# Cross-attention, second layer: the softmax denominators from a split, rounded sum, one key tile later

## What is computed

```python
q = rmsnorm((hidden_states @ Wq).reshape(B, Sq, H, D), gq)
k = rmsnorm((encoder_hidden_states @ Wk).reshape(B, Skv, H, D), gk)
v = (encoder_hidden_states @ Wv).reshape(B, Skv, H, D)
scores = jnp.einsum('bqhd,bkhd->bhqk', q, k) * scale
attn = jax.nn.softmax(scores, axis=-1)
out = jnp.einsum('bhqk,bkhd->bqhd', attn, v)
```

## Time and profile before

| | before |
|---|---|
| median of 3 runs | 2175.83 us |
| profiled execution, its own time | 2174.4 us |
| its span, first to last instruction | 2172.6 us |
| mean granted TensorE clock | 0.998 |
| second layer's attention | about 1397 to 1980 us of the span |
| one batch of it (sums to sums) | 34.3 to 34.4 us |

### The profile page before, as it was taken

The page is one execution under the profiler, slowest core; times in us unless marked ns, Lnnn a source line. Parts: engine busy times, 40 slices in busy tenths (PEclk is TensorE's granted clock), DMA queues, the critical chain, the costliest instruction groups (busy, mean ns, idle before and its releaser), DMA issues. The chain is left out here.

```text
span 2172.6 us, 27566 instructions
## 1 busy us (share of the span) xinstructions
PE 2110.9 (97%) x8962; PEld 1571.2 (72%) x8962; DVE 1575.4 (73%) x2592; ACT 972.9 (45%) x2593; POOL 1409.9 (65%) x1120
## 2 busy tenths in 40 slices
PE   7999999999999999999999988999999999999999
PEld 7777777777777777777777556666666666665998
DVE  4889888898889888988896642556665666652677
ACT  3444445545454445444545337544444344431432
POOL 1468776887778777877787237187878787771221
PEclk9999999999999999999999999999999999999999
DMA  3000000000000000000001410011011111101110
GB/s 132 29 15 16 29 29 15 21 23 29 15 29 15 29 19 25 15 29 29 15 10 40 140 46 1 29 43 57 29 57 30 56 49 37 43 1 52 37 52 25
DMA packets 15136, 75.63 MB, mean 35 GB/s; under 512 B 1746, under 2 KB 2114, under 8 KB 13986
## 3 DMA queue, kind: packets, MB, share of 16 engines
q1 hardware_dynamic: 14994, 73.89, 10.4%
HBM read 72.97 MB, written 0.92 MB: 34 GB/s over the span
## 5 line engine op out<-in xcount | busy, mean ns | idle before, releaser
L612 POOL TENSOR_TENSOR l_prod<-l_prod 125x256 f32<-125x256 f32 x576 | 417.4, 738 | 270.4 <-DVE l_prod L677 269.7
L677 DVE TENSOR_TENSOR l_prod<-l_side,xq 125x512 f32<-125x512 f32 x576 | 394.9, 686 | 56.2 <-PE l_side L809 48.3
L954 POOL TENSOR_TENSOR l_acc<-l_acc,l_probs 125x896 f32<-125x896 f32 x160 | 346.0, 2162 | 81.7 <-ACT l_probs L904 66.0
L553 ACT ACTIVATE l_probs<-l_slots,mask_bias 125x448 f32<-125x448 f32 x384 | 237.8, 632 | 340.6 <-PE l_slots L748 340.5
L974 DVE TENSOR_TENSOR l_scaled<-l_slots,rk 125x896 f32<-125x896 f32 x192 | 207.0, 1085 | 197.8 <-PE l_slots L1039 197.7
L606 POOL TENSOR_TENSOR l_acc<-l_acc,l_probs 125x896 f32<-125x896 f32 x160 | 338.6, 2116 | 0.0
L535 ACT ACTIVATE l_prod_act<-l_prod_act 125x128 f32<-125x128 f32 x768 | 228.0, 298 | 235.3 <-DVE l_prod_act L677 235.3
L904 ACT ACTIVATE l_probs<-l_scaled 125x896 f32<-125x896 f32 x192 | 182.8, 952 | 320.7 <-DVE l_scaled L974 296.8
L686 DVE TENSOR_REDUCE l_msq<-l_prod 125x4 f32<-125x256 f32 x576 | 235.0, 410 | 1.7
L640 DVE SCALAR_TENSOR_TENSOR top<-l_side,mask_bias,top 125x448 f32<-125x448 f32 x330 | 223.4, 677 | 6.8 <-PE l_side L792 5.8
L1037 PE MATMUL l_slots<-l_qhi,l_clo 128*125 128x448 f32 x384 | 203.0, 529 | 1.4 <-DVE l_qlo L979 1.4
(11 more groups left out here) (258 smaller groups left out, 4487.9 us busy)
## 6 DMA issues: line engine op xcount, KB each, us to landing
land<-in_ctxT SPq DMA_DIRECT2D x32, 750.0 KB, 4.3
l_nat<-in_ctxN SPq DMA_DIRECT2D x16, 750.0 KB
post_we<-in_experts SPq DMA_DIRECT2D x20, 384.0 KB, 3.0
spare<-in_ctxN SPq DMA_DIRECT2D x8, 750.0 KB
nat<-in_ctxN SPq DMA_DIRECT2D x8, 750.0 KB
spare<-in_wo SPq DMA_DIRECT2D x2, 2048.0 KB, 8.5
spare<-in_wqT SPq DMA_DIRECT2D x4, 512.0 KB, 9.2
mid_fac<-in_factors SPq DMA_DIRECT2D x1, 2048.0 KB, 8.2
```

The source lines that it names most:

```text
L553: act.activation(P[t % NP][:, HALF * i:HALF * i + HALF], bank_of("S", t, i)[0:KT, 0:HALF], ACT.Exp, bias=m.mask_bias[:, b, t:t + 1]).then_ ...
L612: pool.tensor_tensor(buf[:, :, 0:C // 2], buf[:, :, 0:C // 2], buf[:, :, C // 2:C], ALU.add).then_inc(s.half_sum, 1)
L677: dve.tensor_tensor(to[:, :, :], bank, xt.unsqueeze(1).to_broadcast([KT, 4, C]), ALU.mult).then_inc(s.side_dve, 1)
L954: pool.tensor_tensor(acc[:, :], acc[:, :], P[t % NP][:, :], ALU.add).then_inc(s.acc, 1)
```

## The change

The denominators are no longer taken from acc by a plain float32 matmul. ScalarE rounds acc to float32r (acc_hi), GpSimd subtracts to get the remainder (acc_lo), and TensorE makes two float32r matmuls for each half, with a float32r block of ones (one). On ScalarE the rounding stands behind exp of tile 1 of the next batch and ahead of `values_out`; on GpSimd the remainder stands ahead of `low_parts` and the adds of the next batch; on TensorE `sums` moves from step 0 to step 1, and on VectorE `invert` and `normalise` from steps 0 and 1 to steps 1 and 2.

```diff
         acc = sb("acc", [KT, QW], F32)
+        acc_hi, acc_lo = sb("acc_hi", [KT, QW], F32R), sb("acc_lo", [KT, QW], F32R)
+        one = sb("one", [KT, 128], F32R)
...
+            def sum_high(b):
+
+                act.wait_ge(s.acc, (NT - 1) * (b + 1))
+                need(act, s.den, b)
+                act.activation(acc_hi[:, :], acc[:, :], ACT.Copy).then_inc(s.acc_hi, 1)
...
                     for bt, tt in tile_ahead(LAG, b, t):
                         exp(bt, bt % 2, tt)
+                sum_high(b)
                 values_out(b)
...
             high_parts(0, 0)
+            act.activation(one[:, :], m.ones[0:KT, :], ACT.Copy).then_inc(s.one, 1)
...
                 if t == 1:
 
-                    need(pool, s.den, b)
+                    need(pool, s.acc_lo, b)
                     pool.tensor_tensor(acc[:, :], P[0][:, :], P[1][:, :], ALU.add).then_inc(s.acc, 1)
...
+            def sum_low(b):
+
+                pool.wait_ge(s.acc_hi, b + 1)
+                need(pool, s.den, b)
+                pool.tensor_tensor(acc_lo[:, :], acc[:, :], acc_hi[:, :].bitcast(F32), ALU.subtract).then_inc(s.acc_lo, 1)
...
                     if t == (6 if b == 0 else 0) and nxt:
                         low_parts(b + 1, 1 - par)
+                sum_low(b)
...
-                    if t == 0 and not start:
+                    if t == 1 and not start:
                         invert(b - 1)
-                    if t == 1 and not start:
+                    if t == 2 and not start:
                         normalise(b - 1)
...
             def sums(b):
 
-                pe.wait_ge(s.acc, (NT - 1) * (b + 1))
+                pe.wait_ge(s.acc_lo, b + 1)
+                pe.wait_ge(s.one, 1)
                 need(pe, s.inv, 2 * b)
...
                 for half in range(2):
-                    last = pe.matmul(norm_banks[:, half, 0:HALF], m.ones[0:KT, :], acc[:, HALF * half:HALF * half + HALF],
-                                     start=True, stop=True)
+                    cols = slice(HALF * half, HALF * half + HALF)
+                    pe.matmul(norm_banks[:, half, 0:HALF], one[:, :], acc_lo[:, cols], start=True, stop=False)
+                    last = pe.matmul(norm_banks[:, half, 0:HALF], one[:, :], acc_hi[:, cols], start=False, stop=True)
                 last.then_inc(s.den, 1)
...
-                        if half == 1 and t == 0 and not start:
+                        if half == 1 and t == 1 and not start:
                             sums(b - 1)
```

More of the change, by code:

```diff
@@ L842, in second_attention @@
         "ld_land", "ld_nat0", "ld_nat1", "ctx_hi", "ctx_lo", "q_hi", "q_lo", "scores", "scaled", "probs", "pv", "acc",
-        "den", "inv", "o_raw", "o_done", "fold_pe", "fold_act", "fold_dve", "y_pe", "y_act"])
+        "one", "acc_hi", "acc_lo", "den", "inv", "o_raw", "o_done", "fold_pe", "fold_act", "fold_dve", "y_pe", "y_act"])
     LAG, NP = 2, 3
```

## The result

The changed kernel takes 2190.95 us (median of four runs, 2189.8 to 2193.53) against 2175.79 before (the three runs given above and one more): ratio 1.0072, 95% interval 1.0056 to 1.0088. It is 15.2 us slower, where +13.65 was forecast; the forecast time was 2189.5. The profiled execution took 2191.12 us with a span of 2189.3, 16.7 over the 2172.6 of before.

What follows compares the result with a forecast made beforehand. TensorE, busy 34.4 of 34.4 us a batch, bounds the kernel. Per boundary 1.44 + 0.18 + 0.82 - 1.51 = +0.93, times 15, less 0.3, gives +13.65: 2189.5 us, range 2184.5 to 2195, widened to 2182 to 2199.

Steps and rivals of the forecast that it cites:

- The saving on TensorE: In sums on TensorE: two float32 matmuls (1.51) become four float32r ones (0.82), a gain of 0.69 a batch.
- The stall for the copy: At each boundary TensorE's products of tile 0 wait for ScalarE's copy out of psO: a new stall of 1.44.
- The reciprocals: On VectorE, reciprocals start later against TensorE, whose stall grows from 0.10 to 0.28: 0.18 more a boundary.
- acc_lo and the first adds: On GpSimd: remainder ready 1.5 us ahead of sums, exp of tile 3 with 1.3 cover; nothing on the path.
- The rule on the port: On VectorE, normalise may be held to the end of GpSimd's third add: cost 0, with 0.3 left.
- The rival built on it: GpSimd's queue binds: remainder 2.8, normalise blocked by a full add; up to 0.7 a boundary, 2200 us; chance 0.10.
- The sum: Over the attention: +0.93 at each of 15 boundaries, +13.95, less 0.3 at the end, gives +13.65 us.
- The end: Behind the loop: the last sums starts 0.4 later and is 0.69 shorter, -0.3.
- The clock: TensorE's clock stays at 1.00; rival: it falls in the 1.44 wait, 2.73 more a boundary, +41, 2230 us; chance 0.03.

Runs made afterwards that it cites:

- The two runs that move only one piece: Kernel before with sums, invert and normalise one tile later, 2188.06 us; changed kernel with the rounding ahead of exp of tile 1, 2178.84 us.
- moving alone: Kernel before with sums, invert and normalise one tile later, plain float32 sums kept: 2188.06 us against 2177.31, ratio 1.0044.
- The second rounding: Changed kernel with an extra rounding of acc, to a buffer nobody reads, ahead of the first on ScalarE: 2222.15 us, one run.
- one reciprocal a step: Changed kernel with rounding ahead of exp of tile 1, sums in step 0 (acc_hi matmuls first), reciprocals in steps 0 and 1, normalise in step 2: 2178.02 us.
- copy first: Changed kernel with the copy out of psO ahead of the rounding on ScalarE: 2230.57 us, one run.
- copy first with normalise later: Changed kernel with the copy out of psO ahead of the rounding, and the halves of normalise in steps 3 and 4: 2180.56 us, ratio 1.0018.
- both apart: Changed kernel with rounding ahead of exp of tile 1, sums in step 0, reciprocals in steps 0 and 1, normalise halves in steps 2 and 3: 2165.36 us.

## Why the prediction was right

*The saving on TensorE*: 0.81 for the four float32r matmuls, forecast 0.82. Right.

*The stall for the copy*: 1.50, forecast 1.44; the hand-over and the unloaded weights cost 0.21, where I took 0.15. The two runs that move only one piece divide it: 0.66 from the lost cover (moving alone), 0.84 from the rounding ahead of the copy. The second rounding added another 0.8 where the clock held.

*The reciprocals*: 0.30, forecast 0.28; a difference of 0.20 against 0.18.

*acc_lo and the first adds*: hidden, as forecast, with 1.6 and 1.4 us left (forecast 1.5 and 1.3).

*The rule on the port*: the forecast had `normalise` held to the end of the third add and nothing lost by it. It lasted 1.51, 0.36 more than before, and TensorE didn't wait behind it. The Trainium skill, "SBUF — State Buffer", "Who interferes with whom", has a VectorE instruction with two SBUF inputs contend with a GpSimd instruction that reads SBUF, over a port pair that it calls an exclusive lock; the trace agrees, here and more so in the runs with 3.05, 4.22 and 4.98. The rival built on it didn't come true in the changed kernel, but its direction is borne out by two others. Its condition was wrong: the remainder takes 2.08, and what sets it off is where the adds fall against `normalise`. Its size, up to 0.7 a boundary, fits the run with one reciprocal a step and is too small for the one with the copy first (over 1 us in the clean batches).

*The sum*: the 15 boundaries took 15.2 for 13.95, 1.00 each as a rule, because the stall was 0.06 and the reciprocals 0.02 more than forecast (the first interval between copies is 0.1 longer). The end gave 0.43, forecast 0.3, so the attention cost 14.8 for 13.65. The 1.5 us of lower clock behind it belongs to that execution.

*The clock*: it stayed at 1.00 over the attention, as forecast with 0.97. But the ground given, that one idle stretch of 1.41 had done no harm, says less than it seemed to: 0.8 us more of waiting brought it down behind twelve of fifteen boundaries. So the chance of 0.03 had too little behind it, and that the clock held is in part luck; where between 1.26 and 2.10 of idle time it begins to fall, no run shows. The price was wrong too: where the clock fell it cost 1.6 to 1.8 a boundary, and not the 2.73 that the rival had.

## What to carry to other kernels

An operation on the busiest engine can be the cover of another engine's work; before making it shorter or moving it, write down who finishes under it. Put new work of a second engine into a gap that its timeline shows (ScalarE had 1.5 us idle one instruction earlier) and not in front of what the busiest engine waits for next. After any move, look at the VectorE operations with two SBUF inputs and ask what GpSimd runs at that moment.

## What the runs showed of the hardware

`normalise`, two instructions of 448 columns, lasts 0.61 us each where GpSimd is idle. Its means were 0.77, 1.47, 1.60, 1.92 and 2.03 in the changed kernel, the copy first with normalise later, both apart, one reciprocal a step, and copy first. The instructions are the same each time; what differs is which of GpSimd's adds run beside them. No run takes the adds away and leaves `normalise` where it is, so this rests on the times. The copy-first run has them one by one, the first half of `normalise` in the long batch and in the clean one, each with the add beside it:

```profile
1494.41 2.57 DVE L1012 TENSOR_TENSOR qs<-l_inv,qs 128x448 f32<-128x448 f32 x1
1494.38 2.11 POOL L964 TENSOR_TENSOR l_acc<-l_acc,l_probs 125x896 f32<-125x896 f32 x1
```

```profile
1533.83 0.61 DVE L1012 TENSOR_TENSOR qs<-l_inv,qs 128x448 f32<-128x448 f32 x1
1533.83 2.58 POOL L964 TENSOR_TENSOR l_acc<-l_acc,l_probs 125x896 f32<-125x896 f32 x1
```

Where the add had started 0.03 us sooner, it took its usual 2.11 and the multiplication ended 0.49 behind it (0.48 or 0.49 is what this and the changed kernel show for every half that is held). Where both started at 1533.83, the multiplication took its 0.61 and the add 2.58. In each of the nine long batches both halves were held so, in each of the five clean ones one of them was not; a few hundredths of a microsecond decide between a batch of 35.8 us and one of over 39.

TensorE's granted clock stayed at the upper level (2.4 GHz) with 1.26 us of waiting at each of 15 boundaries. With 2.10 us it fell to 1.2 GHz behind twelve of 15, and with 2.8 to 2.9 us (copy first) behind all nine. The shorter wait costs its stall alone, 1.50; the 2.10 mostly 1.6 to 1.8 us besides.
